# First norm of a two-layer GNN: the centring of the rows on VectorE instead of GpSimd

## The reference

```python
h = relu(layernorm(x))                      # (x - mean) / sqrt(var + 1e-5) over 64 features
x = x + segment_sum(mlp(h[row], h[col]), row)
h = relu(layernorm(x))
x = x + gin(h, src, dst)                    # neighbour sum, two-layer MLP, batch norm, relu, + h
```

## Time and profile before

| | us |
|---|---|
| median of 3 runs | 2215.23 |
| lowest, highest | 2206.49, 2216.25 |
| the profiled execution | 2211.46 |
| its span, first to last instruction | 2209.4 |
| VectorE busy | 1076.6 (49%) |
| GpSimd busy | 1052.3 (48%) |
| ScalarE busy | 967.3 (44%) |
| TensorE busy, matmuls | 1494.2 (68%) |

### The profile page before, as it was taken

The page is one execution under the profiler, slowest core; times in us unless marked ns, Lnnn a source line. Parts: engine busy times, 40 slices in busy tenths (PEclk is TensorE's granted clock), DMA queues, the critical chain, the costliest instruction groups (busy, mean ns, idle before and its releaser), DMA issues. The chain is left out here.

```text
span 2209.4 us, 37024 instructions
## 1 busy us (share of the span) xinstructions
PE 1494.2 (68%) x10067; PEld 1073.5 (49%) x10067; DVE 1076.6 (49%) x3310; ACT 967.3 (44%) x2310; POOL 1052.3 (48%) x1004
## 2 busy tenths in 40 slices
PE   0011139999999999999999996255655555555566
PEld 0011127777777777777777775133323233333344
DVE  6899944454444544454444445133333333333344
ACT  0366656666566666666666664011111111111144
POOL 0699954444344343443434331656655565555500
PEclk9999999999999999999999998677777777677775
DMA  1333333434343343434334343222222222222249
GB/s 29 98 117 128 119 91 87 103 80 107 74 107 86 95 102 80 107 87 94 92 89 108 75 107 74 39 48 50 51 42 48 48 45 48 47 45 46 41 143 323
DMA packets 341012, 187.84 MB, mean 85 GB/s; under 512 B 281563, under 2 KB 307560, under 8 KB 340966
## 3 DMA queue, kind: packets, MB, share of 16 engines
q1 hardware_dynamic: 292388, 129.09, 22.5%
q0 software_dynamic: 28224, 32.57, 8.5%
q10 hardware_dynamic: 20354, 25.65, 3.2%
HBM read 131.42 MB, written 55.79 MB: 85 GB/s over the span
## 5 line engine op out<-in xcount | busy, mean ns | idle before, releaser
L784 POOL DMA_INDIRECT fast_gathered<-h_table,fast_gather_i x441 | 420.8, 954 | 625.4 <-PE bank L928 409.0
L1112 POOL DMA_INDIRECT fast_gathered<-h_neighbours_table,fast_index_i x441 | 423.0, 959 | 326.5 <-issue 228.4
L1020 ACT ACTIVATE fast_h<-bank,b_s 128x384 f32<-128x384 f32 (+1 forms) x490 | 300.8, 622 | 330.3 <-PE bank L939 196.5
L1208 ACT ACTIVATE fast_z_in<-node_sums 128x512 f32<-128x512 f32 x49 | 29.3, 597 | 637.4 <-DMA h_table<-prep_normed 621.4
L1193 PE MATMUL bank<-fast_z_in,gw_s 128*128 128x512 f32 x98 | 97.6, 1098 | 298.4 <-ACT fast_z_in L1208 171.9
L1027 ACT ACTIVATE fast_h<-fast_h 128x384 f32<-128x384 f32 (+1 forms) x490 | 273.8, 559 | 0.0
L816 DVE TENSOR_TENSOR fast_message<-bank,b_s 128x192 f32<-128x192 f32 x147 | 52.5, 357 | 437.8 <-PE bank L974 294.9
L1162 DVE BATCH_NORM_STATS2 z_stats<-z_t (+1 forms) x48 | 33.3, 694 | 400.3 <-ACT z_t L1219 290.1
L953 PE MATMUL bank<-fast_h,w_s 128*128 128x384 f32 (+1 forms) x490 | 223.0, 537 | 0.5 <-ACT fast_h L1027 0.5
L928 PE MATMUL bank<-fast_dst_hot,fast_own_rows 128*64 128x128 f32 x1568 | 203.3, 278 | 0.0
L989 PE MATMUL node_sums<-fast_message,fast_hot 128*128 128x80 f32 x1568 | 202.0, 278 | 0.0
(11 more groups left out here) (231 smaller groups left out, 2873.3 us busy)
## 6 DMA issues: line engine op xcount, KB each, us to landing
fast_local<-local_rows SPq DMA_DIRECT2D x49, 576.0 KB
h_neighbours_table<-fast_h_rows SPq DMA_DIRECT2D x49, 320.0 KB
fast_self_rows<-h_neighbours_table SPq DMA_DIRECT2D x49, 320.0 KB
h_table<-prep_normed ACTq DMA_DIRECT2D x49, 256.0 KB, 2.3
fast_own_rows<-h_table SPq DMA_DIRECT2D x49, 256.0 KB
x_plus_h<-fast_x SPq DMA_DIRECT2D x49, 256.0 KB
finish_resid<-x_plus_h SPq DMA_DIRECT2D x49, 256.0 KB
prep_xin<-in_x SPq DMA_DIRECT2D x48, 256.0 KB
```

The source lines that it names most:

```text
L784: pool.indirect_dma_start(gathered[slot][:, j * D:(j + 1) * D], None, h0_t, bass.IndirectOffsetOnAxis(ap=gather_i[q][:, n:n + 1], axis=0))\
L1020: A(to[at][:, 0:w], psum[:, 0:w], ACT.Exp, bias=b_s[:, :]).then_inc(done, 1)
L1112: pool.indirect_dma_start(gathered[q][:, c * MW:(c + 1) * MW], None, h1_t, bass.IndirectOffsetOnAxis(ap=index_i[q][:, c:c + 1], axis=0))\
```

## The change

`centre` leaves GpSimd's stream and goes to VectorE's, as the last body of a step. Its waits (the mean of the block, and the normalise of four blocks before) go with it; its operation and its operands are the same.

```diff
--- before.py
+++ after.py
@@ -545,13 +545,7 @@
                                             f[:, :, 2:2 + K].unsqueeze(2).to_broadcast([128, RAW, CT, K]),
                                             ALU.mult).then_inc(spread_ready, 1)
 
-                        def centre(b, q, turn):
-                            hold(pool, mean_done, b + 1, passed_pool)
-                            wait_from(pool, normed_done, b - RING + 1, passed_pool)
-                            G.tensor_tensor(groups(centred[q][:, :], D), groups(xin[q][:, :], D),
-                                            mean[q][:, :].unsqueeze(2).to_broadcast([128, SUBS, D]),
-                                            ALU.subtract).then_inc(centred_done, 1)
-                        rounds(pool, [(0, centre), (0, spread_fields)], BLOCKS)
+                        rounds(pool, [(0, spread_fields)], BLOCKS)
 
                     @block.vector
                     def _(dve):
@@ -583,8 +577,15 @@
                             V.tensor_reduce(var[q][:, :], groups(squared[q][:, :], D), AX.X, ALU.add)\
                              .then_inc(var_done, 1)
 
+                        def centre(b, q, turn):
+                            dve.wait_ge(mean_done, b + 1)
+                            wait_from(dve, normed_done, b - RING + 1)
+                            V.tensor_tensor(groups(centred[q][:, :], D), groups(xin[q][:, :], D),
+                                            mean[q][:, :].unsqueeze(2).to_broadcast([128, SUBS, D]),
+                                            ALU.subtract).then_inc(centred_done, 1)
+
                         dve.wait_ge(const_made, 3)
-                        rounds(dve, [(0, sum_columns), (2, variance), (0, mean_of_sum), (0, row_hots)], BLOCKS)
+                        rounds(dve, [(0, sum_columns), (2, variance), (0, mean_of_sum), (0, row_hots), (0, centre)], BLOCKS)
 
                         dve.wait_ge(packed_copied, BLOCKS)
                         f = groups(packed[:, :], K)
```

## The result

| | before | after |
|---|---|---|
| median us | 2211.56 (2206.49 to 2216.25, 4 runs) | 2252.58 (2248.34 to 2257.00, 4 runs) |
| profiled execution us, span | 2211.46, 2209.4 | 2248.34, 2246.4 |
| first row one-hots of prepare, start | 75.53 | 75.81 |
| last row one-hots, start | 288.44 | 324.65 |
| first load of the next phase | 303.14 | 341.21 |

The ratio is 1.0186 (95% interval 1.0152 to 1.0221): slower by 41 us on the medians, by 37 us on the two profiled executions. The phase "prepare" accounts for that: from the first row one-hots to the next phase's first load it takes 265.4 us instead of 227.6, 37.8 more, and what follows takes 1905.2 us instead of 1906.3 (each is the span less the start of that load).

What follows compares the result with a forecast made beforehand. VectorE, excluding and excluded by GpSimd, was taken to bound prepare: block 3.82 + 0.82 + 0.56 = 5.20 us. Phase 35.4 plus end 2.8 gave +38.2 on 2211.46, 2249.7; median forecast 2251, own range 2243 to 2259, wider range 2230 to 2262.

Steps and rivals of the forecast that it cites:

- What bounds the phase: In prepare, VectorE has no idle gap and sets the pace, 4.405 us a block; its two-input operations and GpSimd's exclude each other.
- The undisturbed block of 3.82 us: VectorE's own work in a loop block, start to start, without centring or waits: 0.60 + 0.59 + 0.07 + 0.23 + 2.33.
- Who goes first behind the row one-hots: At the row one-hots' end the waiting spread runs 0.82 us, then the centring ends 0.56 us behind it; 5.20 us a block.
- The sum: From first to last row one-hots 249.1 us instead of 212.9; their end 35.4 us later; with the phase's end +38.2.
- The end of the phase: The last square waits for the last centring, so unpacking starts 4.68 us behind the row one-hots, 2.8 us more than before.
- The centring's price: Each of 49 centrings on VectorE takes 0.68 us, bounds 0.67 and 0.74, adding 0.60 us if undisturbed.
- The register write: In the loop, between row one-hots and centring, coming with the centring's wait: costs nothing, upper bound 0.1 us.
- The mean: In the loop it waits behind GpSimd's spread, 0.74 us instead of 0.15; the 0.59 us is given back after the change.
- VectorE keeps the turn: Rival: the centring goes first behind the row one-hots, spread beside sum and variance; block 4.42, 2211 to 2215 us; chance 0.12.
- GpSimd gets in before the row one-hots: Rival: row one-hots take 3.26 us, the centring follows undisturbed; block 5.27 us, total 2254 us; chance 0.04.
- The mean still waits: Rival: the centring's own 0.60 us is added to the 4.405 us block; 2243 us with the end; chance 0.02.
- the release of the x buffers, ScalarE and the loads have slack enough: In prepare, x buffers freed four blocks back and ScalarE's 2.97 us of work against 5.20 a block add nothing.

Runs made afterwards that it cites:

- the block with the centring out of the spread's way: Changed kernel with the centring on VectorE moved between variance and mean; block 4.42 to 4.43 us, 1996.34 us, ratio 0.9996 to the kernel before.
- The two experiments that move the centring: Changed kernel with VectorE's centring put ahead of the tile one-hots (ratio 1.0033) or between variance and mean (0.9996), ratios to the kernel before.
- The doubled spread: Changed kernel with each spread done twice on GpSimd, the first into an unread buffer; 2034.45 us, ratio 1.0189 to the kernel before.
- the last three kernels: Without centring (ratio to the kernel before 1.0001); also with a buffer for the last x and sum's square later (0.9957); also ScalarE's move behind normalise (0.9954).
- The mean on ScalarE: Kernel before the change with the mean's scaling moved from VectorE to ScalarE; 2007.12 us, ratio 1.0049 to the kernel before.
- a later experiment: Changed kernel with centring removed, ScalarE squaring and normalising x itself with a bias, variance from sum of squares; 2198.89 us, ratio 1.0001 to the kernel before.
- the two kernels with the last x apart: No-centring kernel with an own buffer for the last block's x and sum's square one block later (2190.30 us); also ScalarE's move behind the normalise (2187.29 us).

## Why the prediction was right

*What bounds the phase* (VectorE's stream, and the exclusion between its two-input operations and GpSimd's): right but for one word. "Two-input" is too narrow. The mean's scaling has one tensor as input, and it waits as well: 0.74 us in 41 of the 49 blocks of the kernel before, 0.15 to 0.17 in all 49 after, where no GpSimd operation runs beside it. The undisturbed block of 3.82 us was read off two blocks of the kernel before; the block with the centring out of the spread's way came out at 3.82 + 0.60 = 4.42, measured 4.42.

*Who goes first behind the row one-hots* was the step on which everything hung, and the one place where the trace of before had a single clean case (79.10 us in the earlier trace rows). To build 49 blocks on one case was a risk, which the chance of 0.12 for the other order shows. It held 49 times out of 49. Forecast: spread's end 0.82 us behind the row one-hots, centring's 0.56 behind that, recorded with 1.46; measured 0.82, 0.55, 1.45. Block forecast 5.20, measured 5.19 to 5.20. The two experiments that move the centring show that this meeting, and not the centring's own work, is the loss: 0.78 us a block of the 1.38 are the meeting. The doubled spread fits the rule behind it, that turns alternate.

*The sum.* The last row one-hots' end: forecast 327.1, measured 327.06. That this fits to the hundredth is luck: the first row one-hots started at 75.81 instead of 75.53, and the way from there to the last took 248.84 us instead of 249.1, two misses of about 0.3 us that cancel. The end of the phase: forecast 2.8 us later against that, measured 4.63 - 1.89 = 2.74. First load of the next phase: forecast about 341, measured 341.21. Total on the profiled executions: forecast +38.2, measured +36.9 (the rest of the kernel varied by about 1 us the other way). Median: forecast 2251, measured 2252.58; the forecast was set between two figures and not summed, and the four runs lie between 2248.34 and 2257.00, so the closeness says little.

*The centring's price*, 0.68 us: the changed kernel shows it only inside the 1.45; 0.67 and 0.69 in the two kernels that move it. *The register write*: nothing, as taken; the centring starts 2.33 to 2.34 us after the row one-hots' start in the blocks written out and in the loop alike. Among the short operations of the last three kernels the loop did add time, so the zero holds for this place and not for every one.

*The mean.* Its duration fell to 0.15 us as forecast. But the way I put it, that the loop "pays 0.59 us more for the mean that waits", reads as if this were a price of its own. The mean on ScalarE shows that it isn't: without it the wait stands at the one-hots. It did no harm to the forecast, because there the spread, the only partner left, lay wholly behind the row one-hots.

*The rivals.* "VectorE keeps the turn" is out, by all 49 centrings at 1447 ns or more. "GpSimd gets in before the row one-hots" is out, by row one-hots of 2418 ns at most. "The mean still waits" is out, by a mean of 0.15 us. That the release of the x buffers, ScalarE and the loads have slack enough held here, but for the loads it was a matter of what frees the buffers: when a later experiment tied them to the normalise, the last load, which needs over 7 us, cost 4 us.

## What to carry to other kernels

Taking work from GpSimd to a full VectorE is not priced by its duration. List the operations of both engines that exclude each other, in the order in which they come. In these runs a waiting GpSimd operation went in at the first end of an excluding VectorE operation, so what should follow there is an operation that takes no part (here a reduction), and not a second one that does. Tell from the trace which operations take part, not from the number of their inputs: here the one-input scaling of 8 elements did. And when an operation's duration is far above the same operation's elsewhere in the trace, look for the partner that it waits for before counting on getting that time back.

## What the runs showed of the hardware

- VectorE's two-input operation and GpSimd's multiply took turns when both had one waiting: row one-hots, spread, centring, spread, each ending 0.82 us (GpSimd) or 0.55 us (the 512-element centring) behind the other, in 49 blocks of the kernel with the doubled spread, although VectorE's next operation was issued 0.08 us before the last one's end.
- VectorE's reductions of 512 elements kept their 0.67 to 0.69 us beside a GpSimd operation; its one-input scaling of 8 elements did not (0.74 us instead of 0.15).
- A wait of this sort can move without shrinking: with the mean on ScalarE, its 0.59 us came up as 0.10 us in the tile one-hots and 0.77 us in the row one-hots, and the phase took 9 us more.
- In the two kernels with the last x apart, where three VectorE operations of about 0.16 us follow one another, a block took 4.03 to 4.06 us written out, 4.14 to 4.15 in the loop and 4.28 to 4.30 at the loop's turn. In the changed kernel, with one such operation, the block took 5.19 to 5.20 us in either form.
- A normalise of 64 elements on ScalarE with a scale and a bias from memory took 425 ns in the median, with a scale from memory alone 332 ns.
- The same program ran at 1996.78 us on one chip and at 2198.70 to 2211.56 on others, with TensorE's mean granted clock at 0.935 and 0.883; the durations on VectorE in the phase were the same (row one-hots 2.41 to 2.42 us).
